# Graph attention walks with filler matmuls, target logits from three bf16 pieces, and self loops joined per node

## The reference, cut to what matters

```python
h = einsum('nd,dhf->nhf', x, W)                  # 8 heads of 32
al_s, al_d = sum(h * a_src, -1), sum(h * a_dst, -1)
logits = leaky_relu(al_s[src] + al_d[dst], 0.2)
m = segment_max(logits, dst)
e = exp(logits - m[dst])
z = segment_sum(e, dst)
out = segment_sum(h[src] * (e / (z[dst] + eps))[..., None], dst)
```

## Time and profile before

| | |
|---|---|
| median of 3 runs | 7869.34 us |
| span of the profiled execution, first to last instruction | 7089.8 us |
| median less that span (launch and what lies around the instructions) | 779.5 us |
| PE / DVE / POOL / ACT busy, share of the span | 77 / 57 / 41 / 34 % |
| mean granted TensorE clock | 0.796 |
| the four walks | about 643 to 647 us each |

### The profile page before, as it was taken

One profiled execution on the slowest core, in us unless ns is written; L12 is line 12 of the kernel. 1 busy time (PEld: TensorE's weight loads), 2 busy tenths in 40 slices (PEclk: granted clock), 3 DMA queues, 4 the chain that ended last, 5 costly groups with the idle time before them and its releaser, 6 DMA issues. The chain is left out here.

```text
span 7089.8 us, 85054 instructions
## 1 busy us (share of the span) xinstructions
PE 5426.1 (77%) x21265; PEld 3965.8 (56%) x21266; DVE 4048.3 (57%) x8410; ACT 2394.9 (34%) x5747; POOL 2934.6 (41%) x2894
## 2 busy tenths in 40 slices
PE   0788759458886678875888488888979998476998
PEld 0566436346664555654666344446768887354776
DVE  5466733356664447764777577762147776794112
ACT  0333212123332133332333255542205554362333
POOL 1566432336660056644666277760007776000000
PEclk9666659766667866766766699998989999796999
DMA  3433323233440044433334111110019999461000
GB/s 89 124 115 116 70 79 110 80 93 114 117 103 12 2 123 114 117 93 98 115 115 100 41 30 32 31 19 18 7 48 345 353 357 254 120 196 16 9 13 23
DMA packets 455428, 710.74 MB, mean 100 GB/s; under 512 B 105113, under 2 KB 334039, under 8 KB 455015
## 3 DMA queue, kind: packets, MB, share of 16 engines
q0 software_dynamic: 142432, 380.88, 19.8%
q1 hardware_dynamic: 310442, 318.36, 14.1%
q10 hardware_dynamic: 2304, 8.52, 0.3%
HBM read 604.94 MB, written 102.97 MB: 100 GB/s over the span
## 5 line engine op out<-in xcount | busy, mean ns | idle before, releaser
L653 POOL DMA_INDIRECT l_edges_stage<-l_h_rows,src_t x832 | 831.9, 1000 | 463.5 <-issue 238.9
L890 PE MATMUL l_edges_ps_sum<-l_edges_msg,l_edges_hot 128*128 128x264 f32 x1664 | 741.2, 609 | 172.2 <-DVE l_attn_acc L764 157.1
L2086 POOL DMA_INDIRECT l_edge_kv<-l_kv_rows,src_t x416 | 465.1, 1118 | 741.0 <-POOLq L1999 557.2
L2522 POOL DMA_INDIRECT l_gate_edges_srow<-l_gate_src_rows,l_gate_edges_idx x512 | 567.6, 1109 | 251.4 <-issue 155.8
L890 PEld LDWEIGHTS l_edges_ps_sum<-l_edges_msg,l_edges_hot 128*128 128x128 f32 x1664 | 446.4, 291 | 373.2 <-DVE l_attn_acc L764 276.9
L2656 PE MATMUL l_gate_edges_ps<-l_gate_edges_wide,l_gate_edges_hot_lo 128*128 128x500 f32 x1024 | 487.0, 633 | 127.3 <-DVE l_gate_edges_wide L2584 127.3
L653 POOL DMA_INDIRECT l2a_edges_stage<-l2a_h_rows,src_t x416 | 414.0, 995 | 236.8 <-issue 114.7
L653 POOL DMA_INDIRECT l2b_edges_stage<-l2b_h_rows,src_t x416 | 413.2, 993 | 237.4 <-issue 116.8
L890 PE MATMUL l2b_edges_ps_sum<-l2b_edges_msg,l2b_edges_hot 128*128 128x272 f32 x832 | 355.3, 581 | 87.6 <-DVE l2b_attn_acc L764 79.8
L890 PE MATMUL l2a_edges_ps_sum<-l2a_edges_msg,l2a_edges_hot 128*128 128x272 f32 x832 | 353.9, 579 | 87.6 <-DVE l2a_attn_acc L764 77.7
L2656 PEld LDWEIGHTS l_gate_edges_ps<-l_gate_edges_wide,l_gate_edges_hot_lo 128*128 128x128 f32 x1024 | 204.9, 205 | 369.6 <-issue 214.5
(11 more groups left out here) (745 smaller groups left out, 11376.6 us busy)
## 6 DMA issues: line engine op xcount, KB each, us to landing
l_val_rows<-l_edge_vj SPq DMA_DIRECT2D x104, 512.0 KB, 5.7
l_agg_stage<-l_val_rows SPq DMA_DIRECT2D x52, 1024.0 KB, 5.3
l_edge_ea<-in_edge_attr SPq DMA_DIRECT2D x388, 128.0 KB, 5.1
l_edges_rel_b<-rel_rows SPq DMA_DIRECT2D x52, 512.0 KB, 4.0
l_experts_w<-in_L_ffn_w SPq DMA_DIRECT2D x32, 512.0 KB, 4.6
l_gate_edges_lo_b<-l_gate_edges_lo_rows SPq DMA_DIRECT2D x64, 256.0 KB, 3.2
l_edges_stage<-l_h_rows,src_t POOLq DMA_INDIRECT x832, 2.8
l2a_edges_rel_b<-rel_rows SPq DMA_DIRECT2D x26, 512.0 KB, 4.0
```

Of the source, the lines that this page charges most:

```text
L653: nc.gpsimd.indirect_dma_start(out=stage[:, c % 2, u, :], out_offset=None, in_=h_rows, in_offset=bass.IndirectOffsetOnAxis(ap=K.src_t[:, c ...
L890: nc.tensor.matmul(ps_sum[u][:], hot[:, g, u, :], msg[:, g % 2, u, :], start=True, stop=True).then_inc(summed, 1)
L2086: nc.gpsimd.indirect_dma_start(out=kv[:, m, u, :], out_offset=None, in_=kv_rows, in_offset=bass.IndirectOffsetOnAxis(ap=K.src_t[:, n * EB ...
L2522: nc.gpsimd.indirect_dma_start(out=srow[:, n % 4, u, :], out_offset=None, in_=src_rows, in_offset=bass.IndirectOffsetOnAxis(ap=idx[:, n * ...
```

## The change

The edits are these:

1. PE gets 34 products a chunk whose result nobody reads (`keep_warm`: weights and moving data are ones in bf16, 256 columns, into a PSUM buffer of its own): 5 behind turn_logits, 5 behind place_ends, 5 behind place_tops, 5 behind scatter 3, 14 behind expand.
2. The target logits are kept as three bf16 pieces (`adp`, a piece and twice the rest), and `hotT` is written as bf16. A tile's expansion is one bf16 product of 24 columns. DVE sums the three pieces by a reduction of its own (`ad`) before `z`.
3. The walk leaves self loops out. It carries each target's maximum instead of the loop's weight in the last 8 columns, and `finish_gat` joins the loop per node with two exponentials. `own` and `joined` leave the walk.
4. `place_f` comes ahead of `turn_maxima`. The small PE results of a chunk share one PSUM buffer.

```diff
 def project(...)
+                near = h[:, :, RW:RW + HEADS]
+                left = near
+                for j in range(PIECES):
+                    piece = adp[:, 0:NT, j, :]
+                    ch.link(nc.vector.tensor_copy(piece, left))
+                    if j + 1 < PIECES:
+                        ch.link(nc.vector.tensor_tensor(rest[:], left, piece, ALU.subtract))
+                        left = rest[:]
 def gat_edges(...)
-        hotT = ph.sb("hotT", [P, CK * P])
+        hotT = ph.sb("hotT", [P, CK * P], BF16)
-        ps_ad = ph.psum("ps_ad", [P, CK, AW])
+        ps_ad = ph.psum("ps_ad", [P, CK, PIECES, HEADS])
...
                 def logits(c, j, m):
                     dve.wait_ge(expanded, c + 1)
+                    nc.vector.tensor_reduce(ad[:], ps_ad[:].rearrange("p k j h -> p k h j"), AX.X, ALU.add).then_inc(dv, 1)
                     dve.wait_ge(gathered[m], j * (16 * CK) + 16 * CK)
-                    nc.vector.tensor_tensor(z[:], stage[:, m, :, HW:RW], ps_ad[:, :, 0:HEADS], ALU.add).then_inc(dv, 1)
-                    if loops:
-                        nc.vector.tensor_tensor(own[:, m], ps_ad[:, :, HEADS:AW], bcast(K.lastb_t[:, bass.ds(c * CK, CK)], HEADS), ALU.add).then_inc(dv, 1)
...
+                    nc.vector.tensor_tensor(z[:], stage[:, m, :, HW:RW], ad[:], ALU.add).then_inc(dv, 1)
...
                     if loops:
-                        nc.vector.tensor_tensor(own_x[:, m], own[:, m], by_edge, ALU.subtract)
+                        nc.vector.tensor_tensor(last_max[:, m], by_edge, bcast(K.last_t[:, bass.ds(c * CK, CK)], HEADS), ALU.mult)
...
+                def keep_warm(n):
+                    for _ in range(n):
+                        nc.tensor.matmul(ps_warm[:], K.warm[:, 0:P], K.warm[:], start=True, stop=True)
...
                     scatter(c, 0)
                     if after >= 1:
                         turn_logits(c + 1, 1 - m)
+                    keep_warm(5)
                     scatter(c, 1)
                     if after >= 1:
                         place_ends(c + 1)
+                    keep_warm(5)
                     scatter(c, 2)
                     if after >= 1:
                         place_tops(c + 1)
+                    keep_warm(5)
                     scatter(c, 3)
                     if after >= 2:
                         blks = block_ids(nc, mybir.EngineType.PE, K, c + 2)
+                    keep_warm(5)
                     if after >= 1:
+                        place_f(c + 1)
                         turn_maxima(c + 1)
-                        place_f(c + 1)
                     if after >= 2:
                         expand(c + 2, m, blks)
+                    keep_warm(14)
 def finish_gat(...)
-                    ch.link(nc.vector.tensor_tensor(own, own, bcast(w, HC), ALU.mult))
-                    ch.link(nc.vector.tensor_tensor(body, body, res[:], ALU.add))
+                    ch.link(nc.vector.tensor_tensor(share[:, 1], r[:], own[:], ALU.max))
...
+                    ch.note(nc.vector.tensor_tensor(flat.rearrange("p t (h c) -> p t h c", c=C), by_head[:, :, :, 0:C], bcast(share[:, 0], C), ALU.mult))
                     dve.wait_ge(own_in, 16)
...
+                    ch.note(nc.vector.tensor_tensor(mine, mine, bcast(share[:, 1], C), ALU.mult))
...
+                    ch.link(nc.vector.tensor_tensor(by_row, by_row, mine, ALU.add))
```

More of the change, by code:

```diff
@@ L400, in _ @@
                 pe.wait_ge(kready, 1)
-                for n, frm in enumerate((rel, bad, None, idc, lastb)):
+                for n, frm in enumerate((rel, bad, None, idc, last)):
                     if n:
                         pe.wait_ge(tab_copied, n)
-                    if frm is lastb:
+                    if frm is last:
                         pe.wait_ge(lready, 1)
@@ L407, in _ @@
                         rows_of = rows[:, g, 0, :] if frm is None else frm[:, g, :]
-                        last = nc.tensor.transpose(ps_tab[:, g * KP:(g + 1) * KP], rows_of, K.ident[0:KP, 0:KP])
-                    last.then_inc(tab_done, 1)
+                        turned = nc.tensor.transpose(ps_tab[:, g * KP:(g + 1) * KP], rows_of, K.ident[0:KP, 0:KP])
+                    turned.then_inc(tab_done, 1)
 def norm_stats(nc, dve, ch, y, ph, stats_done, var_ready, std_ready, eps, stat, mean, rstd, a, b):
@@ L611, in gat_edges @@
         lg = ph.sb("lg", [P, 2, CK, HEADS])
-        own = ph.sb("own", [P, 2, CK, HEADS]) if loops else None
-        own_x = ph.sb("own_x", [P, 2, CK, HEADS]) if loops else None
-        joined = ph.sb("joined", [P, CK, HEADS]) if loops else None
+        ad = ph.sb("ad", [P, CK, HEADS])
+        last_max = ph.sb("last_max", [P, 2, CK, HEADS]) if loops else None
         local = ph.sb("local", [P, 2, P])
@@ L664, in _ @@
             def _(dve):
-                SEG2 = 3 if loops else 1
+                SEG2 = 2
                 STEP = SEG2 + 2 + 2 + 2
@@ L855, in expand @@
                     for u in range(CK):
-                        last = nc.tensor.matmul(ps_ad[:, u, :], hotT[:, u * P:(u + 1) * P],
-                                                adn[:, bass.ds(blks[u], 1), :].rearrange("p a h -> p (a h)"), start=True, stop=True)
+                        last = nc.tensor.matmul(ps_ad[:, u].rearrange("p j h -> p (j h)"), hotT[:, u * P:(u + 1) * P],
+                                                adp[:, bass.ds(blks[u], 1)].rearrange("p a j h -> p (a j h)"), start=True, stop=True)
                     last.then_inc(expanded, 1)
@@ L861, in turn_logits @@
                     pe.wait_ge(lg_made, c + 1)
-                    frm = joined[:] if loops else lg[:, m]
-                    nc.tensor.transpose(lgT, frm.rearrange("p k h -> p (k h)"), K.ident[:]).then_inc(lg_turned, 1)
+                    nc.tensor.transpose(lgT, lg[:, m].rearrange("p k h -> p (k h)"), K.ident[:]).then_inc(lg_turned, 1)
                 def place_ends(c):
@@ L915, in _ @@
                 place_tops(0)
+                place_f(0)
                 turn_maxima(0)
-                place_f(0)
                 expand(1, 1, block_ids(nc, mybir.EngineType.PE, K, 1))
@@ L1152, in _, with finish_gat @@
                 ch.link(nc.vector.tensor_tensor(K.x[:], K.x[:], acc[:, 0:NT, 0:D], ALU.add))
-def finish_gat(nc, K, name, acc, eps, bias, out, relu=False, add=True, own_rows=None):
+def finish_gat(nc, K, name, acc, eps, bias, out, relu=False, add=True, own_rows=None, own=None):
     with Phase(nc, name) as ph:
@@ L1214, in gat_layer @@
     with Phase(nc, name + "_attn") as keep:
-        adn = keep.sb("adn", [P, NT + 1, AW])
+        adp = keep.sb("adp", [P, NT + 1, PIECES, HEADS], BF16)
+        own = keep.sb("own", [P, NT, HEADS]) if loops else None
         with Phase(nc, name + "_nodes") as nodes:
@@ L1219, in gat_layer @@
             norm_and_transpose(nc, K, name + "_norm", src_x, xn, xnT, norm)
-            project(nc, K, name + "_proj", xnT, w_view, att, att_heads, h_rows, adn)
+            project(nc, K, name + "_proj", xnT, w_view, att, att_heads, h_rows, adp, own)
         acc = keep.sb("acc", [P, NT + 1, HW + (HEADS if loops else 0)])
-        gat_edges(nc, K, name + "_edges", h_rows, adn, acc, loops)
-        finish_gat(nc, K, name + "_fin", acc, eps, bias, dst_x, relu, add, h_rows if loops else None)
+        gat_edges(nc, K, name + "_edges", h_rows, adp, acc, loops)
+        finish_gat(nc, K, name + "_fin", acc, eps, bias, dst_x, relu, add, h_rows if loops else None, own)
 GT = 5
```

101 lines of the change are left out of this document (56 added, 45 removed).

## The result

The changed kernel takes 8184.39 us (median of 4 runs, 8172.82 to 8194.21) beside 7880.51 for the kernel before: a ratio of 1.0387, 95% interval [1.0351, 1.0423]. It is 3.9% slower, where 7547 and a faster kernel were forecast.

A forecast was written before the change was run, and what follows sets the result against it. Bound: a PE-to-DVE-and-back ring, four times a chunk, neither engine alone. Walks save 311 us and finish_gat 11, together 322 off 7869.3: 7547 us, range 7470 to 7670.

The forecast's parts named there:

- That part lies around the instructions, and I take it as unchanged: Whole kernel: the 779.5 us between profiled span (7089.8) and median (7869.34) lie outside the span and stay.
- Behind place_tops (1.11): DVE's third wait for PE in a chunk, 1.11 us: about 0.2 us stays once small records run at the upper clock.
- POOL's wait for messages gone: Sign to look for: POOL's wait for the next chunk's messages falls from 3.4 to under 0.7 us.
- The rival "slower": Walks: fillers do not raise the clock and PE becomes the bound, 28.6 us a chunk, 8360 us; chance 0.04.
- Clock 0.9 or more in the walks: Sign to look for: the walks' granted clock, 0.65 in the profile, rises to 0.9 or more.
- The rival in which it falls once a chunk: Walks: the clock still falls once a chunk, giving 21.8 us a chunk, about 7660 us; chance 0.13.
- Filler 0.15 us: PE: price of each filling product, taken as 0.15 us between ends of 0.11 and 0.227.
- Waits 1 to 3: DVE's waits behind turn_logits (2.17), place_ends (1.32) and place_tops (1.11): zero, zero and about 0.2 us stay.
- hotT to x 2.15: DVE's fourth wait in a chunk: the stretch from hotT's start to x stays, 2.06 us before and 2.15 after.
- DVE's ring 20.1: Walks: DVE's work and remaining waits for PE fall from 23.75 to 20.1 us a chunk, including 0.66 for `ad`.
- Gathers take over, 20.65: Walks: gathers set the pace at 20.45 us a chunk, 20.65 with 0.2 added for stretches where the clock falls.
- finish_gat: Joining own rows after the walks of 2a and 2b: 9 us less in 2a, 2.3 less in 2b.

The follow-up runs named there:

- e15_before: Kernel before plus asserted bounds on PE's expert-table read, profiled on a chip where before takes 7860.83 us: 7891.22 us.
- e1_before: Kernel before plus asserted bounds on PE's expert-table read, on a chip where before takes 7086.83 us: 7114.25 us, ratio 1.0043.
- after: The changed kernel itself, in its first timing and profile beside a before of 7880.51 us: 8184.39 us, ratio 1.0387.
- e10_after: The changed kernel plus asserted bounds on PE's expert-table read, on a chip where before takes 7087.99 us: 6847.61 us, ratio 0.9659.
- e7_nofill: The changed kernel without its filling products, on a chip where before takes 7087.99 us: 7050.01 us.
- e9_half: The changed kernel with every second gather left out (zeros instead, another output), where before takes 7087.99 us: 6703.85 us.

## Why the prediction was wrong

*The step that failed first* is the opening one: "That part lies around the instructions, and I take it as unchanged". The 779.5 us lay inside the span. e15_before against e1_before: the spans differ by 789 us, the four walks (first to last `z`) by 3035 - 2380 = 655, and the other 134 lie in other stages, which no run took apart. The profile was of a chip without the stall and the times of one with it. A gap of a tenth between an execution and the median should have been a warning, not a constant.

*The step that gave the sign*: "Behind place_tops (1.11)" and "About 0.2 stays". On a chip without the stall 0.17 us stay, which is right. On the chip timed, 11.0 us stay in 96 of the 100 chunks. No row ahead could show that. The walks there: before 3035 us (e15_before), changed 3347 (after, on another chip), 312 more; the result is 304 more.

*Why the change made it worse there* is the part that I had argued for as a gain. Messages now come quickly enough that POOL never waits inside a run ("POOL's wait for messages gone"). That closed the breaks through which PE's signals had come. The rival "slower" (fillers at the lower level, 28.6 us a chunk) named another mechanism, and did not occur: fillers hold the clock, 0.95 in e10_after against 0.65 in e7_nofill. That the measured time, 8184, lies between the forecast and that rival's 8360 says nothing for it.

The other steps are judged by e10_after, with 7114 for before:

- Clock 0.9 or more in the walks: 0.95. The level falls five times in the 25 intervals of block 1's walk. The rival in which it falls once a chunk, which I drew from the Trainium skill (TensorE: Matmul & The Clock Gate, A second HAM failure mode), did not come.
- Filler 0.15 us: 5 take 0.72 and 14 take 1.69 in the timeline, so 0.108 more for each, and my choice was high. The trace agrees with the 0.109 that I had worked out from N / 2.4 GHz + 2.5 ns in the Trainium skill (TensorE: Matmul & The Clock Gate, Wait — 56ns, not 53.3ns?).
- Waits 1 to 3 gone but 0.2: 0, 0, 0.17. Expansion 1.1 to 2.2: 1.31.
- hotT to x 2.15: 2.76. The missed term is PE's register load of the block ids (1.11 us in the trace, begun at scatter 3's last product), of which 0.58 us lie open before the fillers:

```profile
1573.95 2.84 PE L895 MATMUL l_edges_ps_sum<-l_edges_msg,l_edges_hot 128*128 128x264 f32 x8
1577.37 0.71 PE L855 MATMUL l_edges_ps_warm<-warm 128*128 128x256 bf16 x5 [0.58 <-issue]
```

- DVE's ring 20.1: 20.01 over block 1's walk in e9_half. That it agrees so well is luck, two misses that cancel. hotT to x grew by 0.8 us where 0.1 was counted. The reduction `ad`, counted at 0.66, takes 0.55 but adds nothing: from weigh 0 to `z` 2.27 us pass before and 2.29 in e9_half (means of 20 chunks), as `z` had stood idle for 0.47 of them before.
- Gathers take over, 20.65: right in kind, 21.25 in size. Intervals of `z` alternate between 20.4 and 21.1 (20.75, where I had 20.45). Every seventh is 22.3 or 22.4, and in each of these three POOL stands 1.8 to 2.4 us between two gathers for nothing recorded. The last is 26.5.

```profile
1606.57 0.94 POOL L660 DMA_INDIRECT l_edges_stage<-l_h_rows,src_t  x1 [1.82 <-issue]
```

- Walks 311 less: 2380 - 2129 = 251.
- finish_gat, last add to the end of the combined rows: 2a 37.2 to 28.1 us, 9.1 less (forecast 9); 2b 40.9 to 39.1, 1.8 less (2.3). In 2b a small operation, not the early product, stood still beside POOL's addition (the last section has the rows).

Together 322 were forecast and 267 measured. With 267 taken from 7880 the forecast would still have been off by 570 us: the stall is the whole of the miss in sign.

**What stays open.** Why PE's signals are held back on these chips while gathers are issued in a row. The Trainium skill (NOTIFIC — the notification-queue block, 7.1 Overflow: three behaviours, one of which stalls the engine) says that the unit that writes the records of events, when its ring is full, drops the new record, overwrites the oldest or stalls the producer. Lost records would fit the missing half, most of it of DMAs, and a stalled producer would fit signals that come late by the number of gathers and not by their bytes, since each gather raises its semaphore 16 times. No run shows either link. Every execution here was recorded, so no run tells whether the stall would be there without recording; that is the rival most worth a test.

## What to carry to other kernels

Compare a profile's span with the times it stands beside before using it; if they differ by more than a per cent or two, the profile is of another situation. On some chips a run of back-to-back GpSimd gathers went with late semaphore updates of another engine (10.6 us in a run of 16, 1.5 us with pauses after 8): look at whether the run is broken, and expect a change that feeds GpSimd without pause to bring the wait out. Where several chips are in use, the version with pauses is the safer one: 7393 where before takes 7861, and some 7250 where before takes 7087, an estimate from 6848 + 100 x (25.3 - 21.3). That is some 2% slower than before there, so the version without pauses is best where the stall is absent.

## What the runs showed of the hardware

- On three of six chips PE's semaphore updates came up to 14 us late in a run of 16 gathers. In `after` hardly any of PE's updates that fall beside the first four gathers of a run is over 1 us late, a third beside the fifth, and nearly all from the seventh to the last. With runs of 8 and 2.6 us of pause the wait at place_tops was 1.5 us, though the expansion's update still came 5.9 us late; with runs of 2 and 4 the wait was 0.2 us. Before's broken runs go with less as well (3.5 us in runs of 12, 8.5 in runs of 16).
- The size of a gather hardly matters to it: with 32 bytes a row a stalled chunk waited 9.6 us, with 1088 it waited 11.0.
- In 2b a DVE operation of 200 elements a lane, 0.37 us in 2a, took 12.82 us beside POOL's bias addition (13.65 us). DVE's timeline in e10_after:

```profile
3673.75 12.82 DVE L1215 TENSOR_TENSOR l2b_fin_share<-l2b_fin_share,l2b_fin_r 128x200 f32<-128x200 f32 x1
3686.50 0.35 DVE L1216 TENSOR_TENSOR l2b_fin_share<-l2b_fin_share,l2b_fin_r 128x200 f32<-128x200 f32 x1
```

POOL's addition starts at 3672.70 and ends at 3686.35, and the DVE operation ends 0.2 us behind it. The Trainium skill (SBUF — State Buffer, SBUF: two separate sides) has an exclusive lock between a GpSimd operation that reads SBUF and a VectorE instruction with two SBUF inputs; the trace agrees. In the earlier trace rows the large product took 3.5 us more; here the small one took the wait.
